# Mixture attention on one Trainium2 core: the gate exponential behind the copy of turned probabilities, the row maximum ahead of the output sums

## The reference

```python
n1 = _layernorm(x, ln1_w, ln1_b)
rw = _gating(n1.reshape(b * t, c), smha_sim, smha_gates, MIN_ATT).reshape(b, t, -1)
q = jnp.einsum('btc,ech,bte->bth', n1, q_proj, rw)      # k and v alike
scores = jnp.einsum('bth,bsh->bts', q, k) * scale
scores = jnp.where(causal, scores, -jnp.inf)
attn = jnp.einsum('bts,bsh->bth', jax.nn.softmax(scores, axis=-1), v)
attn_out = jnp.einsum('bth,ehc,bte->btc', attn, o_proj, rw)
hs = x + attn_out
```

## Time and profile before

| | |
|---|---|
| median of 3 runs | 3327.19 us (3326.01 to 3327.84) |
| profiled execution | 3325.49 us, span 3323.60 us |
| PE busy | 3024.0 us (91% of the span) |
| PEld busy | 2619.5 us (79%) |
| DVE busy | 2447.1 us (74%) |
| ACT busy | 1841.4 us (55%) |
| POOL busy | 1492.6 us (45%) |
| mean granted TensorE clock | 0.963 of 2.4 GHz |

### The profile page before, as it was taken

One profiled execution on the slowest core, in us unless ns is written; L12 is line 12 of the kernel. 1 busy time (PEld: TensorE's weight loads), 2 busy tenths in 40 slices (PEclk: granted clock), 3 DMA queues, 4 the chain that ended last, 5 costly groups with the idle time before them and its releaser, 6 DMA issues. The chain is left out here.

```text
span 3323.6 us, 86059 instructions
## 1 busy us (share of the span) xinstructions
PE 3024.0 (91%) x26992; PEld 2619.5 (79%) x26992; DVE 2447.1 (74%) x6657; ACT 1841.4 (55%) x6739; POOL 1492.6 (45%) x1682
## 2 busy tenths in 40 slices
PE   3999999869999999999599999999979999998878
PEld 2777777658888888888499999999977777776756
DVE  5888888766666666666567777777768888887544
ACT  2777777744444444444334444444437777776534
POOL 1444444435565656656432222222214544544456
PEclk9999999979999999999899999999989999999579
DMA  5000000010000000000000000000010000000244
GB/s 198 17 13 16 13 16 13 1 53 10 9 9 8 9 9 8 9 9 9 30 14 10 13 9 12 10 9 13 4 42 17 13 16 13 16 13 1 73 131 144
DMA packets 55913, 85.93 MB, mean 26 GB/s; under 512 B 6784, under 2 KB 42625, under 8 KB 55042
## 3 DMA queue, kind: packets, MB, share of 16 engines
q1 hardware_dynamic: 47204, 65.65, 6.3%
q0 software_dynamic: 6528, 16.92, 1.4%
q10 hardware_dynamic: 2080, 2.10, 0.2%
HBM read 57.21 MB, written 28.48 MB: 26 GB/s over the span
## 5 line engine op out<-in xcount | busy, mean ns | idle before, releaser
L538 ACT ACTIVATE L_probs<-bank,L_neg_max 128x128 f32<-128x128 f32 x2048 | 722.1, 390 | 263.9 <-DVE L_neg_max L615 263.9
L538 ACT ACTIVATION_READ_ACCUMULATOR L_probs<-bank,L_neg_max 128x1 f32 x2048 | 470.1, 230 | 0.0
L621 DVE COPY L_probsT<-bank 128x512 f32<-128x512 f32 x512 | 351.7, 687 | 125.3 <-PE bank L444 122.2
L1503 ACT ACTIVATE M_inter<-bank 128x512 f32<-128x512 f32 x256 | 153.0, 598 | 435.1 <-PE bank L69 435.1
L67 PE MATMUL bank<-W_hi,M_nT_hi 128*128 128x384 f32 x1024 | 366.6, 358 | 0.3 <-DVE M_qkv L1217 0.3
L615 DVE TENSOR_REDUCE L_neg_max<-bank 128x4 f32<-128x512 f32 x512 | 327.6, 680 | 29.5 <-PE bank L435 29.5
L68 PE MATMUL bank<-W_hi,M_nT_lo 128*128 128x384 f32 x1024 | 346.4, 338 | 0.0
L69 PE MATMUL bank<-W_lo,M_nT_hi 128*128 128x384 f32 x1024 | 346.2, 338 | 0.0
L444 PE MATMUL bank<-constants,L_probs 128*128 128x128 f32 x2048 | 330.7, 284 | 15.3 <-ACT L_probs L538 7.2
L1551 DVE TENSOR_TENSOR M_inter_lo<-M_inter,M_inter_hi 128x512 fp32r<-128x512 f32 x256 | 185.0, 723 | 188.9 <-ACT M_inter_hi L1504 183.3
L67 PE MATMUL bank<-M_nT_hi,W_hi 128*128 128x256 f32 x1024 | 296.5, 290 | 0.0
(11 more groups left out here) (310 smaller groups left out, 9509.9 us busy)
## 6 DMA issues: line engine op xcount, KB each, us to landing
L_ctx_in<-in_ctx SPq DMA_DIRECT2D x64, 256.0 KB, 2.6
M_tile<-M_sorted SPq DMA_DIRECT2D x72, 130.0 KB, 2.4
raw_weights<-in_weights SPq DMA_DIRECT2D x2, 4096.0 KB, 14.2
hs<-M_hs SPq DMA_DIRECT2D x64, 128.0 KB, 1.7
M_hs<-hs SPq DMA_DIRECT2D x32, 256.0 KB, 2.7
x_all<-in_x SPq DMA_DIRECT2D x6, 1024.0 KB, 8.2
M_sorted<-M_fill SPq DMA_DIRECT2D x16, 130.0 KB, 2.4
x_all<-in_x ACTq DMA_DIRECT2D x2, 1024.0 KB, 14.4
```

Source lines behind the costliest of these rows:

```text
L538: last = act.activation(probs[:, k % 2, i, :], score_bank[u][:, i, :], ACT.Exp, bias=neg_max[:, u, i:i + 1], scale=-1.0, accum_out=sums[:, ...
L621: dve.tensor_copy(probsT[:, k % 2], pT_ps).then_inc(pT_ready, 1)
L1503: act.activation(inter[:, e % 2], up_bank[e % 2], ACT.Gelu).then_inc(M.inter_ready, 1)
```

## The change

On ScalarE, in `step`, `gate_exp(s + 2)` moves from ahead of `weigh_odd(s + 1, 1 - b, 5)` and `keep_p(s)` to behind them. On VectorE, in `step`, `row_max(s)` moves from behind `weigh_out(s - 1, 1 - b, 0)` and `weigh_even(s + 1, 1 - b, 2)` to ahead of them. No operation is added or removed, and the other engines' lists stay as they are.

```diff
@@ -1156,11 +1156,11 @@
                     exps(s)
                     if not first:
                         weigh_out(s - 1, 1 - b, 2)
-                    if two:
-                        gate_exp(s + 2)
                     if one:
                         weigh_odd(s + 1, 1 - b, 5)
                     keep_p(s)
+                    if two:
+                        gate_exp(s + 2)
                     if one:
                         weigh_odd(s + 1, 1 - b, 7)
                     round_a(s)
@@ -1269,11 +1269,11 @@
                     if two:
                         rest_n(s + 2, b)
                         guard(s + 2)
+                    row_max(s)
                     if not first:
                         weigh_out(s - 1, 1 - b, 0)
                     if one:
                         weigh_even(s + 1, 1 - b, 2)
-                    row_max(s)
                     if two:
                         gate_first(s + 2)
                     sum_scale(s)
```

## The result

The changed kernel takes 3357.01 us (median of 4 runs, 3355.73 to 3359.32), the kernel before 3326.6 on the same chip: a ratio of 1.0096, 95% interval 1.0078 to 1.0113. It is 30 us slower where 36 us faster was forecast, and it lies outside the range, beyond rival 2 on the slower side. The profiled execution took 3355.73 us (span 3353.9, mean granted clock 0.963 as before).

The account below looks back on a forecast made before the run. TensorE was taken as nearly the bound (busy 746 of 812.76 us), its waits the possible gain. 70 us won less 40 given back, plus 6 outside the loop, made 36 us: 3291 us, range 3242 to 3305.

Parts of the forecast that it names:

- rival 2: VectorE later: L878, not L876, held by the GpSimd instruction after L1330; 1.65 us a step, 3337 to 3342 us; chance 0.11.
- The wait at L1015: TensorE's wait for the copy of the turned probabilities disappears, winning 1.25 us a step, 70 us in the loop.
- VectorE's gap: VectorE idles 1.00 us before L1257; the row maximum (0.28 + 0.08 us) fits there and costs nothing.
- GpSimd's addition: L1339 moves earlier, from 1179.05 to about 1178.5, so L856 starts 0.1 us behind a GpSimd start.
- L856, L860 and L862 were held: VectorE gate operations stand until GpSimd instructions end: L856 to 1179.24, L860 to 1180.12, L862 to 1181.12.
- L1217 at 1181.4: VectorE's weighing starts at 1181.4, after the end of the held L862.
- L876 at 1183.37: VectorE reaches L876 at 1183.6 in the forecast's clock, in the middle of GpSimd's last L1330.
- the price of the last hold: L876 held to about 1183.95 costs TensorE 0.85 us a step at aT_lo; bounds 0 and 1.65.
- the loop's sum: Over 56 loop steps: 70 us won, 40 us given back, 30 us left, a step of 13.97 us.
- The eight steps outside the loop: Steps of the stage outside its loop gain between 0 and 1.25 us each, taken as 6 us together.
- late in nine steps of 56: Before the change TensorE waits 0.91 us for aT_lo, VectorE's last result, in nine steps only.
- each hold ends at a GpSimd end: Argument on VectorE's chain of three holds: each release at a GpSimd end wipes out errors made before it.

Follow-up runs that it names:

- e3_gate_psum: Changed kernel with five 8-column gate tiles in PSUM bank 3, turned probabilities moved to bank 1: 3223.16 us, ratio 0.9671 to the kernel before.
- e1_act_only: Kernel before with only the ScalarE edit, the gate exponential behind the copy, row maximum left in place: 3257.94 us, ratio 0.9772.
- e4_logit_psum: Changed kernel with only the logits gate tile in PSUM, turned probabilities in another bank: 3293.69 us, ratio 0.9817 to the kernel before.

## Why the prediction was wrong

**Step by step, what held.** The wait at L1015 went. The row maximum fitted into VectorE's gap (1174.83, ahead of L1257 at 1175.53). GpSimd's addition moved ahead of L856: forecast 1178.48 and 1178.58, less 0.23 for the shift of the step 1178.25 and 1178.35, measured 1178.27 and 1178.34. L856, L860 and L862 were held (0.69, 0.60, 0.94; forecast 0.66 and about 0.6 and 0.95). L1217 at 1181.4 - 0.23 = 1181.17, measured 1181.17. L876 at 1183.37, measured 1183.28.

**The step that failed** is the one behind it, the price of the last hold: "At 1183.6 it is in the middle of it and is held to its end, about 1183.95 ... It costs TensorE 1.02 - 0.17 = 0.85 us a step at aT_lo". It set L876 against GpSimd's last L1330 at 1182.92, where that instruction would stand if nothing held GpSimd. But GpSimd's second L1330 reads what L1217 writes, and I had just moved L1217 to 1181.4. Worked through with the forecast's own numbers: L1217 ends at 1182.02, the second L1330 runs from 1182.15 to 1183.17, the third from 1183.33 to 1184.35, and L1315 behind it to about 1185.0. L876 then ends at 1184.37, not 1183.95, and L878 is held by L1315 to 1185.05 instead of ending at 1184.15. That is 0.85 + 0.9 = 1.75 us a step; measured were 1.58 and 0.20 (at L1019). With 1.75 the loop's sum is 70 - 98 + 8 = 20 us lost, on the right side of zero.

In the trace of before that link (L1217 to the second L1330) shows no wait: L1217 ends at 1180.96, and GpSimd is busy with the first L1330 until 1181.99. Its slack was 1.03 us, and the held L862, with everything else a microsecond earlier, used it up.

Between 36 us won and 30 us lost lie 66 us. This term makes 52 of them: 88.6 + 11.4 less the 8.2 of before is 91.8 us, where the sum had 40. The wait at L1015 makes 8: it was put at 1.25 us a step, and the loop's loss of 29.7 leaves 62.1 / 56 = 1.11 for it. The eight steps outside the loop make the rest: 6 us won were forecast, and 0.6 were lost.

A reading under it was wrong too. The prediction took aT_lo as late in nine steps of 56. The weight load's row above shows TensorE waiting for it in every step, since L882 is always held, so there was no slack at aT_lo that could have taken up a further hold.

**Rival 2** came nearest: L878 held by the GpSimd instruction behind L1330. Its cause (VectorE 0.3 us later still, and L876 free) was not it. GpSimd came later instead and held L876 too, which is why the price of 3337 to 3342 us was too low. Its chance of 0.11 rested on the thought that "each hold ends at a GpSimd end, which wipes out errors made before it". That holds for errors in VectorE's start, not for a delay that goes round through GpSimd.

**The rule of the ports.** The Trainium skill's page "SBUF — State Buffer", section "Who interferes with whom", has an instruction with at most one SBUF input, outside the two-port modes, free of GpSimd. e3_gate_psum agrees: L878, one of whose two inputs is then in PSUM, takes 170 to 172 ns in all 64 steps, while it took 0.65 us in the changed kernel's row above. The prediction applied the rule rightly to L856, L860, L862 and L876, and did not ask it of L882 and of the copy L1205, which was held in 47 of the 56 steps before (0.69 us in the median, 0.15 by itself). What was missing above all was the way back, from a held VectorE operation to GpSimd's next start.

**ScalarE's half, taken apart.** It won 1.17 us a step (14.51 - 13.34) against 0.77 without holds. The weight loads tell where the 0.40 comes from. At L1015 their wait falls from 74.5 to 12.1 us with the holds and from 56.4 to 12.2 without: L860's 0.32 us a step no longer reaches the copy, once the exponential stands behind it. At L67 it goes from 23.3 to 20.8 with the holds and from 1.8 to 3.1 without, which is the other 0.07. The 0.31 us that e1_act_only still loses to holds (13.34 - 13.03) is that last row, (20.8 - 3.1) / 56 = 0.32: L882 is held in all 56 steps, L878 in five.

**Not shown.** What VectorE's half would do alone without holds; its 0.16 us is measured only on top of ScalarE's half. And why L878 meets GpSimd in nine steps of before and just misses it in others stays open.

## What to carry to other kernels

When an operation is found to be late, follow every reader of it, on the other engine too, before the next time on that engine is used; a semaphore wait that shows no idle time in the trace is still a link, and its slack has to be written down. Where small VectorE operations run beside long GpSimd ones, move their operands to PSUM before tuning the order around them: here that alone turned a change of +30 us into one of -107 us. And judge an edit of the order with the holds taken out; with them in, the two halves gave -72 and +13 us alone and +30 together. When TensorE's row shows no wait, look at its weight loads too, also where the row says "issue": they held the wait that was missed here.

## What the runs showed of the hardware

- A VectorE operation on 8 columns takes 0.15 to 0.28 us by itself, and 1.02 us when a GpSimd instruction of 1.01 us has started just ahead of it (L878 in e4_logit_psum). It is let go 0.02 to 0.03 us after GpSimd's end, and a GpSimd instruction waiting in the list does not get in ahead of it: L876 and L878 of the changed kernel are held one after the other, each once.
- The start decides within hundredths: L878 0.01 us behind is held (1152.43 against 1152.42), 0.10 us ahead it is not. In the kernel before it starts together with L1330, or up to 0.01 us behind, in 19 steps and is free; 0.01 to 0.02 us behind in nine, and is held. L874 is otherwise: in the changed kernel it is held for 1.08 to 1.10 us though its recorded start is 0.04 to 0.05 us ahead of L1330 (28 steps), and free at 0.14 us ahead (the other 28).
- GpSimd itself lost little by it: in the loop steps L1330 takes 1.00 to 1.06 us in the kernel before and 1.01 to 1.03 in the changed one.
- Not every small operation is held. In e1_act_only L864, with one input in SBUF, ran its 0.16 us at 1159.39, inside GpSimd's 1159.35 to 1160.08.
